# Three TensorE steps placed one chunk later, and a last store split by rows over two queues

## The chip, the cores and the metric

One core of one Trainium2 chip runs the whole program. The metric is the device time of one execution in microseconds (us); less is better. The kernel before was timed in three runs, and one further execution was recorded by the profiler.

## What is computed

Four residual stages on x of shape 4 x 512 x 512 (batch, tokens, features), all in fp32. Cut to what matters:

```python
x = x + gelu(_layernorm(x) @ ((w1.T @ w2.T) * sparse_mask) + b2)          # stage 1
x = x + ffn(_layernorm(x))                                               # stage 2
x = x + attention(_layernorm(x))        # stage 3: softmax(q k^T) v, then Wo
x = x + ffn(_layernorm(x))                                               # stage 4

def ffn(x):
    dots = softmax(x @ centroids.T / 0.1)       # 64 clusters, per token
    hits = dots > 0.01
    query_sel = any(hits, axis=1)               # per token
    cluster_sel = any(hits, axis=0)             # over ALL tokens of ALL batches
    row_sel = cluster_sel[assignments]          # per output feature
    return where(query_sel[:, None] & row_sel[None, :], x @ weight.T + bias, 0)
```

In stages 2 and 4 the line with `cluster_sel` matters most: no output of the stage can be finished before the cluster probabilities of every token are known.

## The kernel before

Tokens lie on the 128 partitions. There are 4 batches of 4 token tiles; a tile "b.t" is 128 tokens x 512 features. Each fp32 product is made of three matmuls on a high and a low part of its operands (hi*hi, lo*hi, hi*lo; `products`, line 1012). A tile's 512 x 512 product is cut by its contraction into four chunks of 128, so one chunk is three matmuls of 128x512. The steps of every engine stand in hand-written lists (`PE_ORDER`, `ACT_ORDER`, `DVE_ORDER`, `POOL_ORDER`, and `SP_ORDER` and `AS_ORDER` for the DMA issues of SyncE and ScalarE). Each engine works its own list strictly in order, and a step first waits on semaphores for what it reads and for the buffer it writes. `dn4.2.1.c3` is chunk 3 of the stage 4 product of tile 2.1; `c20` means chunks 2 and 0.

PSUM is split in two rotations of four banks each: `t_bank` for transposes and the masks, `m_bank` for products. A new tile takes the bank of the tile four places earlier in its rotation and waits until that one has been read (`bank_for`, line 1043). In stage 4 the tiles take `m_bank` in the order dn4.2.3, cl4.3, dn4.2.1, dn4.3.0, dn4.3.2, so dn4.3.2 waits for `blend4.2.3`, the VectorE step that reads dn4.2.3 (line 977).

The choice of clusters runs once in stage 2 and once in stage 4, through all engines. For the last batch (3) it is:

- `cl.3` (PE, line 1197): logits against the centroids; `lgev.3` (ACT, line 681): copy out of PSUM to `lg`;
- `tc.3` (PE, line 1119): four transposes of `lg`;
- `logit`, `lmax` (DVE, lines 930 to 937): sum of parts and maximum; `cexp` (ACT, line 703): four exponentials; `prob` (DVE, lines 944 to 954); `best1` (DVE, line 959): the maximum over all batches;
- `bestT` (PE, line 1124): its transpose; `csel` (DVE, lines 965 and 966): the chosen clusters;
- `mask.2` (PE, line 1144) in stage 2; `tmask.4` and `masks.4` (PE, line 1138) in stage 4: the mask of the output features, in PSUM. `tmask.4` is read by VectorE, and `masks.4` is copied by `rows4` (ACT, line 713) to SBUF for Pool.

PE works chunks of products between these steps.

In stage 4 a finished product is blended (`blend4`, DVE, line 977) with what has been prepared in `y_tok`, and then the mask is applied. Twelve tiles get it from VectorE with one `out` step (copy_predicated, line 1001), after Pool has added x to `y_tok` (`xb`, line 559). The tiles in `BY_POOL` (four: 1.3, 2.3, 3.2 and 2.2) get it from Pool instead, with two steps, `pm` (multiply, line 565) and `pa` (add, line 570), and no `xb`. The last tile, 3.3, is worked in two column halves (`dn4h`, `blend4h`, `outh`, lines 988 and 994).

Each tile is stored by one DMA of 256 KB once it is finished; tile 3.3 by two of 128 KB, one for each column half (`storeh`): the first issued by ScalarE (line 763), the second by SyncE (line 391). The last DMA in ScalarE's list is the store of tile 2.2 (line 769). SyncE then waits for all stores (line 434).

Of the kernel before, what the change touches and what calls it, by code (L numbers as in the profile page):

```python
# [24 lines left out]
M_BANKS = 4  # L25
WARM = 12

BY_POOL = {(1, 3), (2, 3), (3, 2), (2, 2)}

SQUARED = {2, 3, 4}  # L30

# [11 lines left out]
y1.3.3.c1 dn2.1.1.c02 y1.3.3.c3 dn2.1.3.c30 tc.2.1 y1.3.2.c1 y1.3.3.c20 y1.3.2.c3 dn2.1.1.c3 y1.3.2.c2  # L43
dn2.1.3.c1 T.x2.2.0 dn2.1.1.c1 dn2.1.3.c2 T.x2.2.2 y1.3.2.c0 y1.3.1.c2 T.x2.2.3 y1.3.1.c13 T.x2.2.1 y1.3.0.c1
y1.3.1.c0 y1.3.0.c302 T.x2.3.3 cl2.2.h01 T.x2.3.2 T.x2.3.1 dn2.2.3.c0 dn2.3.3.c3 dn2.2.3.c3 T.x2.3.0 tc.2.2
dn2.3.3.c1 dn2.2.3.c21 dn2.2.0.c2 cl2.3.h0 cl2.3.h1 dn2.2.2.c3 tc.2.3 dn2.2.2.c1 dn2.2.0.c1 dn2.2.2.c2
dn2.2.0.c03 dn2.3.3.c20 dn2.2.2.c0 bestT.2 dn2.3.1.c2 mask.2 dn2.2.1.c1 dn2.3.2.c3 dn2.3.1.c03 dn2.2.1.c2
dn2.3.2.c20 dn2.3.1.c1 dn2.3.2.c1 dn2.2.1.c0 T.x3.0.3 dn2.3.0.c13 T.x3.0.0 dn2.3.0.c0 T.x3.0.2 dn2.3.0.c2
T.x3.0.1 dn2.2.1.c3 k.0.h1 k.0.h0 q.0.h0 q.0.h1 v.0.h1 T.x3.1.3 v.0.h0 sc.0.0 T.x3.1.2 T.x3.1.1 sc.0.2 T.x3.1.0
# [6 lines left out]
T.p.3.3 wo.2.3 cl4.1.h01 wo.2.2 dn4.1.3.c0 tc.4.1 wo.2.0 dn4.1.0.c32 T.p.3.0 dn4.1.3.c1 dn4.1.0.c0 T.v.3.0  # L56
T.p.3.1 dn4.1.2.c3 dn4.1.3.c32 dn4.1.2.c102 dn4.1.0.c1 T.x4.2.2 T.x4.2.3 T.x4.2.0 wo.2.1 pv.3.h01 dn4.1.1.c012
wo.3.2 wo.3.0 dn4.1.1.c3 T.x4.2.1 wo.3.3 T.x4.3.0 T.x4.3.2 wo.3.1 cl4.2.h01 T.x4.3.1 T.x4.3.3 tc.4.2 dn4.2.3.c2
cl4.3.h0 dn4.2.1.c1 cl4.3.h1 dn4.2.1.c2 tc.4.3 dn4.2.1.c3 dn4.2.3.c1 dn4.2.1.c0 dn4.3.0.c2 dn4.2.3.c0 dn4.3.0.c0
dn4.2.3.c3 dn4.3.0.c31 bestT.4 dn4.3.2.c2 tmask.4 masks.4 dn4.3.2.c031 dn4.2.2.c0123 dn4.3.1.c0123 dn4.2.0.c0123  # L60
dn4h.3.3.0 dn4h.3.3.1
"""

# [45 lines left out]
rden.3 blend4.1.3 lo.p.3.0 lo.p.3.1 x3.2.1 blend4.1.0 blend4.1.2 lo.x4.2.3 olo.3 lo.x4.2.2 lo.x4.2.0 x3.3.2  # L109
x3.3.0 blend4.1.1 lo.x4.2.1 x3.3.3 lo.x4.3.2 x3.3.1 lo.x4.3.0 lo.x4.3.1 logit.4.2 lmax.4.2 lo.x4.3.3 prob.4.2  # L110
logit.4.3 lmax.4.3 prob.4.3 best1.4 blend4.2.3 csel.4 blend4.2.1 blend4.3.0 out.0.1 out.0.0 out.1.1 out.1.0
blend4.3.2 out.0.2 out.0.3 blend4.2.2 out.2.1 out.3.0 out.1.2 blend4.3.1 out.3.1 blend4.2.0 out.2.0
blend4h.3.3.0 outh.3.3.0 blend4h.3.3.1 outh.3.3.1
"""

# [8 lines left out]
bo.0.2 bo.0.1 masked.3.2 bo.0.0 bias2.3.3 bo.0.3 bias2.3.1 masked.3.3 rstd.3.3.3 masked.3.1 rstd.3.3.0 bo.1.0  # L124
rstd.3.3.2 bo.1.1 bo.1.2 rstd.3.3.1 bo.1.3 bo.2.1 bo.3.0 rstd.4.0 xb.0.1 bo.2.0 bo.2.3 xb.0.3 xb.0.2 xb.0.0
rstd.4.1 bo.2.2 bo.3.2 bo.3.3 xb.1.1 bo.3.1 xb.1.2 xb.1.0 rstd.4.2 rstd.4.3 xb.2.1 xb.3.0 xb.2.0 xb.3.3 xb.3.1
pm.1.3 pa.1.3 pm.2.3 pa.2.3 pm.3.2 pa.3.2 pm.2.2 pa.2.2
"""

SP_ORDER = """  # L130
load.x0.0 load.w2.0 load.x0.1 load.x0.2 load.w1.1 load.x0.3 load.w2.1 load.w2.2 load.w1.2 load.w1.3 load.w2.3
load.ffn.1 load.ffn.0 load.cen load.ffn.2 load.sparse.0 load.ffn.3 load.sparse.1 load.sparse.2 load.sparse.3
load.small load.x.1 load.b2 load.xt.1 load.x.3 load.late load.x.2 load.bias load.xt.2 load.xt.3 store.0.1
store.1.1 store.0.2 store.2.1 store.1.2 store.3.1 store.2.0 storeh.3.3.1
"""


# [1 line left out]


AS_ORDER = """
store.0.0 store.1.0 store.0.3 store.1.3 store.3.0 store.2.3 store.3.2 storeh.3.3.0 store.2.2
"""

def steps_of(text):
# [63 lines left out]
def program(nc, x_d, xt_d, w1_d, w2t_d, b2_d, sparse_d, wqkv_d, bqkv_d, wo_d, bo_d, ffn_d, fb_d, cen_d,  # L209
            assign_d, out_d):  # L210
    ctx = ExitStack()
    with ctx:
# [162 lines left out]
        @block.sync  # L375
        def _(sp):
            rows_of = lambda d: d.rearrange("(c p) n -> p c n", p=P)
            for kind, key in SP_STEPS:
                if kind == "store":
                    b, t = key  # L380
                    if key in BY_POOL:
                        sp.wait_ge(*done_at("pa", key))
                    else:
                        sp.wait_ge(*done_at("out", key))
                    sp.dma_start(out_d[b, t * P:(t + 1) * P, :], x_tok[:, b * TPB + t, :]).then_inc(stored, 16)
                    continue
                if kind == "storeh":
                    b, t, h = key
                    cols = slice(h * D // 2, (h + 1) * D // 2)
                    sp.wait_ge(*done_at("outh", key))  # L390
                    sp.dma_start(out_d[b, t * P:(t + 1) * P, cols], x_tok[:, b * TPB + t, cols]).then_inc(stored, 16)
                    continue
                what = key[0]
                if what in ("w2", "w1"):
                    c = key[1]
                    dst, src = (w2_raw, w2t_d) if what == "w2" else (w1_raw, w1_d)
                    sp.dma_start(dst[:, c, :], src[c * P:(c + 1) * P, :]).then_inc(ld[key], 16)
                elif what == "x0":
                    t = key[1]
                    sp.dma_start(x_tok[:, t, :], x_d[0][t * P:(t + 1) * P, :]).then_inc(ld[key], 16)  # L400
                elif what == "sparse":
                    c = key[1]
                    sp.dma_start(sparse[:, c, :], sparse_d[c * P:(c + 1) * P, :]).then_inc(ld[key], 16)
                elif what == "b2":
                    sp.dma_start(b2[:, :], b2_d.rearrange("(a n) -> a n", a=1).broadcast_to([P, D])).then_inc(ld[key], 16)
                elif what == "cen":
                    sp.dma_start(cen_raw, cen_d).then_inc(ld[key], 16)
                elif what == "ffn":
                    c = key[1]
                    sp.dma_start(ffn_raw[:, c, :], ffn_d[c * P:(c + 1) * P, :]).then_inc(ld[key], 16)  # L410
                elif what == "x":
                    b = key[1]
                    sp.dma_start(x_tok[:, b * TPB:(b + 1) * TPB, :], rows_of(x_d[b])).then_inc(ld[key], 16)
                elif what == "xt":
                    b = key[1]
                    if b == 1:
                        sp.wait_ge(*done_at("T", *[("x1", 0, t) for t in every]))
                    elif b == 2:
                        sp.wait_ge(*done_at("flo"))
                    else:  # L420
                        sp.wait_ge(*done_at("xlo", *[(1, t) for t in every]))
                    sp.dma_start(xt_raw[b % 2][:, :, :], rows_of(xt_d[b])).then_inc(ld[key], 16)
                elif what == "small":
                    sp.dma_start(bqkv[:, :], bqkv_d.rearrange("(j p) -> p j", p=P),
                                  allow_slow_non_contiguous=True).then_inc(ld[key], 16)
                    sp.dma_start(assign, assign_d.rearrange("(a n) -> a n", a=1).broadcast_to([P, D])).then_inc(ld[key], 16)
                elif what == "bias":
                    sp.dma_start(bias_f[:, :], fb_d.rearrange("(a n) -> a n", a=1).broadcast_to([P, D])).then_inc(ld[key], 16)
                    sp.dma_start(bo[:, :], bo_d.rearrange("(a n) -> a n", a=1).broadcast_to([P, D])).then_inc(ld[key], 16)
                elif what == "late":  # L430
                    sp.wait_ge(*done_at("alo"))
                    sp.dma_start(wqkv_raw, rows_of(wqkv_d)).then_inc(ld[key], 16)
                    sp.dma_start(wo_raw, wo_d).then_inc(ld[key], 16)
            sp.wait_ge(stored, 16 * sum(kind in ("store", "storeh") for kind, key in SP_STEPS + AS_STEPS))
# [138 lines left out]
        def _(act):  # L573
# [670 lines left out]
```

## Time and profile before

| | us |
|---|---|
| median of three runs | 275.42 (275.40 to 275.84) |
| the profiled execution's own time | 275.24 |
| its span | 273.4 |
| TensorE busy | 268.8 (98% of the span) |
| VectorE busy | 192.2 (70%) |
| ScalarE busy | 177.0 (65%) |
| Pool busy | 163.8 (60%) |

The profile is of one execution. Its instruction rows start at zero at the start of the span. The span is 1.84 us shorter than the execution's own time. The granted TensorE clock is 9 tenths or more in all 40 slices, and 0.999 in the mean. All DMA traffic lies in the first third (loads) and in the last three slices (stores). TensorE's ends are modelled, because its matmuls are pipelined, so the starts of its rows are the better guide: neighbouring rows overlap, and what is read here is the distance from one start to the next.

### The profile page before, as it was taken

To read this page: it belongs to the slowest core of one execution; us is meant where nothing else is said; L and a number is where in the kernel's file an instruction comes from. 1 tells how busy PE (TensorE), PEld (TensorE's weight loads), DVE (VectorE), ACT (ScalarE), POOL (GpSimd) and SP (SyncE) were. 2 spreads that over 40 slices of the span, in tenths; PEclk is the share of its full clock that TensorE was granted. 3 is DMA by queue.
4 is the path that set the end of the run, shared out by engine and by line. 5 is a ranking of instruction groups with operands and counts; after the bars stand their busy time and mean duration, and the time that the engine had idled before them with its cause. 6 is when DMAs were issued, how large, how long until landed. Compare 5 with 4: busy or idle time off the path is not lost.

```text
span 273.4 us, 4428 instructions
## 1 busy us (share of the span) xinstructions
PE 268.8 (98%) x1397; PEld 225.6 (82%) x1397; DVE 192.2 (70%) x406; ACT 177.0 (65%) x359; POOL 163.8 (60%) x196
## 2 busy tenths in 40 slices
PE   8999999999999999999999999999999999999995
PEld 8787888888888888788988888888888888887784
DVE  3988988605935867794478796788447584875994
ACT  3855886455477786448889988779544747577500
POOL 4883988265395491189896993990541247102795
PEclk9999999999999999999999999999999999999999
DMA  7999064800000000000000000000000000000096
GB/s 253 372 362 326 14 219 167 305 4 2 0 0 0 2 0 2 0 2 0 2 0 0 1 4 0 0 2 0 2 2 0 0 2 0 1 2 0 36 361 220
DMA packets 10247, 18.25 MB, mean 67 GB/s; under 512 B 1200, under 2 KB 1968, under 8 KB 10224
## 3 DMA queue, kind: packets, MB, share of 16 engines
q1 hardware_dynamic: 8784, 15.47, 16.2%
q10 hardware_dynamic: 1440, 2.49, 2.5%
q8 instruction: 12, 0.20, 0.3%
q14 instruction: 11, 0.09, 0.1%
HBM read 13.76 MB, written 4.19 MB: 66 GB/s over the span
## 4 chain that ended last, share of the span: by engine, by line
PE 96%; DMA 1%; DVE 1%; POOL 1%; issue 0%; ACT 0%; DVEq 0%; POOLq 0%
PE m_bank L1018 76%; PE t_bank L1113 12%; PE m_bank L1197 6%; PE t_bank L1119 1%; DMA x_tok<-in_L_attn_a_x 1%; PE m_bank L1073 1%; ACT xn_odd L613 0%; PE t_bank L1138 0%; DVE st L817 0%; POOL rstd L471 0%; POOL ve L470 0%; DVE y_tok L988 0%; DVE x_tok L994 0%; PE m_bank L1144 0%; PE t_bank L1124 0%
## 5 line engine op out<-in xcount | busy, mean ns | idle before, releaser
L1018 PE MATMUL m_bank<-ffn_hi,even_hi 128*128 128x512 f32 x96 | 38.9, 406 | 0.0
L1018 PE MATMUL m_bank<-ffn_lo,even_hi 128*128 128x512 f32 x96 | 37.6, 392 | 0.0
L1018 PE MATMUL m_bank<-ffn_hi,even_lo 128*128 128x512 f32 x96 | 37.4, 390 | 0.0
L602 ACT ACTIVATE ones_and_squares<-x_tok,mv 128x512 bf16<-128x512 f32 x44 | 31.6, 717 | 4.1 <-DVE x_tok L921 3.7
L559 POOL TENSOR_TENSOR y_tok<-y_tok,x_tok 128x512 f32<-128x512 f32 x12 | 15.3, 1289 | 25.6 <-ACT y_tok L755 25.6
L539 POOL TENSOR_TENSOR y_tok<-y_tok,bias_f 128x512 f32<-128x512 f32 x16 | 20.6, 1295 | 16.2 <-ACT y_tok L696 16.2
L467 POOL TENSOR_SCALAR ve<-mv 128x1 f32<-128x1 f32 (+1 forms) x20 | 5.3, 264 | 37.9 <-ACT ones_and_squares L602 36.9
L824 DVE TENSOR_TENSOR even_lo<-t_bank,even_hi 128x512 fp32r<-128x512 f32 x24 | 16.2, 684 | 12.8 <-ACT even_hi L645 12.6
L471 POOL TENSOR_TENSOR rstd<-ve,half 128x1 f32<-128x1 f32 (+1 forms) x31 | 23.5, 758 | 2.6
L824 DVE TENSOR_TENSOR odd_lo<-t_bank,odd_hi 128x512 fp32r<-128x512 f32 x28 | 18.8, 686 | 6.4 <-ACT odd_hi L645 6.2
L1018 PE MATMUL m_bank<-odd_hi,wqkv_hi 128*128 128x512 f32 (+1 forms) x60 | 21.5, 358 | 0.0
L1018 PEld LDWEIGHTS m_bank<-ffn_lo,even_hi 128*128 128x128 f32 x96 | 18.0, 188 | 3.9
L1018 PE MATMUL m_bank<-odd_lo,wqkv_hi 128*128 128x512 f32 (+1 forms) x60 | 20.9, 349 | 0.0
L553 POOL TENSOR_TENSOR x_tok<-x_tok,bo 128x512 f32<-128x512 f32 x16 | 20.9, 1322 | 0.0
L1018 PE MATMUL m_bank<-odd_hi,wqkv_lo 128*128 128x512 f32 (+1 forms) x60 | 20.8, 347 | 0.0
L1018 PEld LDWEIGHTS m_bank<-ffn_hi,even_lo 128*128 128x128 f32 x96 | 18.1, 189 | 3.1
L1018 PEld LDWEIGHTS m_bank<-ffn_hi,even_hi 128*128 128x128 f32 x96 | 18.1, 188 | 3.0
L613 ACT ACTIVATE xn_odd<-x_tok,ve,rstd 128x512 f32<-128x512 f32 x20 | 16.1, 811 | 5.8 <-POOL ve L474 5.8
L1018 PE MATMUL m_bank<-attn_hi,odd_hi 128*128 128x512 f32 x48 | 19.5, 406 | 0.0
L1018 PE MATMUL m_bank<-attn_lo,odd_hi 128*128 128x512 f32 x48 | 18.8, 392 | 0.0
L1018 PE MATMUL m_bank<-attn_hi,odd_lo 128*128 128x512 f32 x48 | 18.7, 390 | 0.0
L645 ACT ACTIVATE even_hi<-t_bank 128x512 fp32r<-128x512 f32 x24 | 13.8, 595 | 6.8 <-PE t_bank L1113 6.8
(191 smaller groups left out, 784.8 us busy)
## 6 DMA issues: line engine op xcount, KB each, us to landing
x_tok<-in_L_attn_a_x SPq DMA_DIRECT2D x3, 1024.0 KB, 9.8
xn_odd<-in_L_attn_a_xt SPq DMA_DIRECT2D x2, 1024.0 KB, 7.3
out<-x_tok ACTq DMA_DIRECT2D x8, 256.0 KB, 2.2
out<-x_tok SPq DMA_DIRECT2D x7, 256.0 KB, 2.2
x_tok<-in_L_attn_a_x SPq DMA_DIRECT2D x4, 256.0 KB, 4.1
w_raw<-in_L_attn_a_w SPq DMA_DIRECT2D x4, 256.0 KB, 5.0
xt_other<-in_L_ffn_weight SPq DMA_DIRECT2D x4, 256.0 KB, 5.9
y_tok<-in_L_attn_a_sparse_mask SPq DMA_DIRECT2D x4, 256.0 KB, 6.5
```

What stands on the lines that cost most here:

```text
L467: link(pool.tensor_scalar(ve[:, i:i + k], mv[:, i:i + k, 1], 1.0 / D ** 3, EPS, ALU.mult, ALU.add))
L471: ins = pool.tensor_tensor(rstd[:, i:i + k], ve[:, i:i + k], half[:, 0:k], ALU.pow)
L539: pool.tensor_tensor(y_tok[:, n, :], y_tok[:, n, :], bias_f[:, :], ALU.add).then_inc(done[kind], 1)
L553: pool.tensor_tensor(x_tok[:, n, :], x_tok[:, n, :], bo[:, :], ALU.add).then_inc(done[kind], 1)
L559: pool.tensor_tensor(y_tok[:, n, :], y_tok[:, n, :], x_tok[:, n, :], ALU.add).then_inc(done[kind], 1)
L602: act.activation(squares, x_tok[:, n, :], ACT.Square, bias=sum_of(*key), scale=-float(D), accum_out=mv[:, i, 1:2]).then_inc(done[kind], 1)
L613: act.activation(xn_odd[:, t, :], x_tok[:, n, :], ACT.Identity, bias=nbias[:, i:i + 1], scale=rstd[:, i:i + 1]).then_inc(done[kind], 1)
L645: act.activation(split_of(what, b, t)[0], bank_view(what, bank_of("T", *key)), ACT.Copy).then_inc(done[kind], 1)
L824: dve.tensor_tensor(lo, bank_view(what, bank_of("T", *key)), f32(hi), ALU.subtract).then_inc(done[kind], 1)
L1018: ins = pe.matmul(bank, a, w, start=(first and n == 0), stop=(last and n == count - 1))
L1113: ins = pe.transpose(bank[:, c * r:(c + 1) * r], blk, ident[0:r, 0:r])
L1197: ins = pe.matmul(bank[:, tokens], cen_hl[:, c, :], a[:, c, tokens], start=(c + h == 0), stop=(c == KC - 1 and h == 1))
```

## The change

- `tc.2.3` comes one chunk later: behind `dn2.2.2.c1` instead of ahead of it.
- `tc.4.3` comes one chunk later: behind `dn4.2.1.c3` instead of ahead of it.
- `tmask.4` and `masks.4` come one chunk later: behind chunks 2 and 0 of dn4.3.2 instead of behind chunk 2 alone.
- Tile 2.2 leaves `BY_POOL`. Pool loses `pm.2.2` and `pa.2.2` and gets `xb.2.2`, ahead of `pm.1.3`; VectorE gets `out.2.2`, ahead of `blend4.2.0`. Its store goes from the end of ScalarE's list into SyncE's list, and the store of tile 3.1 goes the other way.
- The second column half of tile 3.3 is stored by two DMAs of 64 KB, of 64 rows each: the upper on SyncE's queue, the lower on ScalarE's. Both wait for the same VectorE step, `outh.3.3.1`.

```diff
-BY_POOL = {(1, 3), (2, 3), (3, 2), (2, 2)}
+BY_POOL = {(1, 3), (2, 3), (3, 2)}
 # PE_ORDER
-dn2.3.3.c1 dn2.2.3.c21 dn2.2.0.c2 cl2.3.h0 cl2.3.h1 dn2.2.2.c3 tc.2.3 dn2.2.2.c1 dn2.2.0.c1 dn2.2.2.c2
+dn2.3.3.c1 dn2.2.3.c21 dn2.2.0.c2 cl2.3.h0 cl2.3.h1 dn2.2.2.c3 dn2.2.2.c1 tc.2.3 dn2.2.0.c1 dn2.2.2.c2
 dn2.2.0.c03 dn2.3.3.c20 dn2.2.2.c0 bestT.2 dn2.3.1.c2 mask.2 dn2.2.1.c1 dn2.3.2.c3 dn2.3.1.c03 dn2.2.1.c2
...
-cl4.3.h0 dn4.2.1.c1 cl4.3.h1 dn4.2.1.c2 tc.4.3 dn4.2.1.c3 dn4.2.3.c1 dn4.2.1.c0 dn4.3.0.c2 dn4.2.3.c0 dn4.3.0.c0
-dn4.2.3.c3 dn4.3.0.c31 bestT.4 dn4.3.2.c2 tmask.4 masks.4 dn4.3.2.c031 dn4.2.2.c0123 dn4.3.1.c0123 dn4.2.0.c0123
+cl4.3.h0 dn4.2.1.c1 cl4.3.h1 dn4.2.1.c2 dn4.2.1.c3 tc.4.3 dn4.2.3.c1 dn4.2.1.c0 dn4.3.0.c2 dn4.2.3.c0 dn4.3.0.c0
+dn4.2.3.c3 dn4.3.0.c31 bestT.4 dn4.3.2.c20 tmask.4 masks.4 dn4.3.2.c31 dn4.2.2.c0123 dn4.3.1.c0123 dn4.2.0.c0123
 dn4h.3.3.0 dn4h.3.3.1
 # DVE_ORDER
-blend4.3.2 out.0.2 out.0.3 blend4.2.2 out.2.1 out.3.0 out.1.2 blend4.3.1 out.3.1 blend4.2.0 out.2.0
+blend4.3.2 out.0.2 out.0.3 blend4.2.2 out.2.1 out.3.0 out.1.2 blend4.3.1 out.3.1 out.2.2 blend4.2.0 out.2.0
 # POOL_ORDER
-pm.1.3 pa.1.3 pm.2.3 pa.2.3 pm.3.2 pa.3.2 pm.2.2 pa.2.2
+xb.2.2 pm.1.3 pa.1.3 pm.2.3 pa.2.3 pm.3.2 pa.3.2
 # SP_ORDER
-store.1.1 store.0.2 store.2.1 store.1.2 store.3.1 store.2.0 storeh.3.3.1
+store.1.1 store.0.2 store.2.1 store.1.2 store.2.2 store.2.0 storer.3.3.0
 # AS_ORDER
-store.0.0 store.1.0 store.0.3 store.1.3 store.3.0 store.2.3 store.3.2 storeh.3.3.0 store.2.2
+store.0.0 store.1.0 store.0.3 store.1.3 store.3.0 store.2.3 store.3.1 store.3.2 storeh.3.3.0 storer.3.3.1
 # in SyncE's program; ScalarE's has the same with act for sp
+                if kind == "storer":
+                    b, t, r = key
+                    rows_r = slice(r * P // 2, (r + 1) * P // 2)
+                    sp.wait_ge(*done_at("outh", (b, t, 1)))
+                    sp.dma_start(out_d[b, t * P + r * P // 2:t * P + (r + 1) * P // 2, D // 2:D],
+                                 x_tok[rows_r, b * TPB + t, D // 2:D]).then_inc(stored, 16)
+                    continue
```

## Rows read from the trace of the kernel before

**Rows 1.** The page's shares of the chain of work that ended last, by engine.
```profile
PE 96%; DMA 1%; DVE 1%; POOL 1%; issue 0%; ACT 0%; DVEq 0%; POOLq 0%
```

**Rows 2.** That chain in order of time: start, length (us), what, instructions.
```profile
249.37 6.15 PE m_bank L1018 x27
```

**Rows 3.** Timeline of TensorE, stage 2: start, length (us), line, operation, shapes.
```profile
107.96 0.39 PE L1018 MATMUL m_bank<-ffn_lo,even_hi 128*128 128x512 f32 x1
108.44 0.63 PE L1119 MATMUL t_bank<-ident,lg 128*128 128x128 f32 x4
...
114.14 0.39 PE L1018 MATMUL m_bank<-ffn_lo,even_hi 128*128 128x512 f32 x1
114.44 0.27 PE L1124 MATMUL t_bank<-ident,best 128*64 128x128 f32 x1
...
115.45 0.47 PE L1144 MATMUL m_bank<-onehot,csel 128*128 128x512 f32 x1
```

**Rows 4.** Timelines of VectorE and ScalarE, stage 2; bracket: idle before, and what ended it.
```profile
109.17 0.69 DVE L930 TENSOR_REDUCE cl<-t_bank 128x256 f32<-128x512 f32 x1 [0.40 <-PE t_bank L1119]
...
112.02 0.42 DVE L944 TENSOR_REDUCE csum<-ce 128x4 f32<-128x256 f32 x1 [0.17 <-ACT ce L703]
...
113.67 0.62 DVE L959 TENSOR_REDUCE best<-best 128x64 f32<-128x256 f32 x1
...
115.07 0.28 DVE L966 TENSOR_SCALAR csel<-t_bank 64x128 fp32r<-64x128 f32 x1
...
110.55 1.44 ACT L703 ACTIVATE ce<-cl,ncmx,rstd 128x64 f32<-128x64 f32 x4 [2.26 <-DVE ncmx L937]
```

**Rows 5.** Timeline of TensorE, stage 4.
```profile
248.27 0.39 PE L1018 MATMUL m_bank<-ffn_lo,even_hi 128*128 128x512 f32 x1
248.74 0.63 PE L1119 MATMUL t_bank<-ident,lg 128*128 128x128 f32 x4
...
255.36 0.27 PE L1124 MATMUL t_bank<-ident,best 128*64 128x128 f32 x1
...
255.73 0.39 PE L1018 MATMUL m_bank<-ffn_hi,odd_lo 128*128 128x512 f32 x1
255.96 0.40 PE L1018 MATMUL m_bank<-ffn_lo,odd_hi 128*128 128x512 f32 x1
256.42 0.70 PE L1138 MATMUL t_bank<-onehot,csel 128*128 128x512 f32 x2
256.96 0.40 PE L1018 MATMUL m_bank<-ffn_hi,odd_hi 128*128 128x512 f32 x1
```

**Rows 6.** Timeline of VectorE, stage 4, around the same steps.
```profile
254.60 0.74 DVE L977 SCALAR_TENSOR_TENSOR y_tok<-m_bank,rq,y_tok 128x512 f32<-128x512 f32 x1
...
255.99 0.28 DVE L966 TENSOR_SCALAR csel<-t_bank 64x128 fp32r<-64x128 f32 x1
...
257.52 2.59 DVE L1001 COPY_PREDICATED x_tok<-t_bank,y_tok 128x512 f32<-128x512 int32 x4
```

**Rows 7.** TensorE's weight loads in the list of waits: us in total, times, longest.
```profile
PEld m_bank L1018 <- DVE y_tok L977: 0.2, 1, 0.2
```

**Rows 8.** Timeline of VectorE, the last 6 us.
```profile
267.40 0.75 DVE L977 SCALAR_TENSOR_TENSOR y_tok<-m_bank,rq,y_tok 128x512 f32<-128x512 f32 x1 [1.09 <-PE m_bank L1018]
```

**Rows 9.** Timelines of Pool, and of ScalarE's and SyncE's DMA issues, near the end.
```profile
254.86 5.05 POOL L559 TENSOR_TENSOR y_tok<-y_tok,x_tok 128x512 f32<-128x512 f32 x4 [2.83 <-ACT y_tok L755]
...
270.43 0.42 ACTq L769 DMA_DIRECT2D out<-x_tok  x1
...
271.33 0.33 SPq L391 DMA_DIRECT2D out<-x_tok  x1
```

**Rows 10.** DMA issues: queue, count, KB each, median us from issue to landing.
```profile
out<-x_tok SPq DMA_DIRECT2D x7, 256.0 KB, 2.2
...
out<-x_tok ACTq DMA_DIRECT2D x1, 128.0 KB, 2.1
out<-x_tok SPq DMA_DIRECT2D x1, 128.0 KB, 1.7
```

More of the change, by code:

```diff
@@ L433, in _ @@
                     sp.dma_start(wo_raw, wo_d).then_inc(ld[key], 16)
-            sp.wait_ge(stored, 16 * sum(kind in ("store", "storeh") for kind, key in SP_STEPS + AS_STEPS))
+            sp.wait_ge(stored, 16 * sum(kind in ("store", "storeh", "storer") for kind, key in SP_STEPS + AS_STEPS))
         @block.gpsimd
@@ L763, in _ @@
                     act.dma_start(out_d[b, t * P:(t + 1) * P, cols], x_tok[:, b * TPB + t, cols]).then_inc(stored, 16)
+                    continue
+                if kind == "storer":
+                    r = key[2]
+                    rows_r = slice(r * P // 2, (r + 1) * P // 2)
+                    act.wait_ge(*done_at("outh", (b, t, 1)))
+                    act.dma_start(out_d[b, t * P + r * P // 2:t * P + (r + 1) * P // 2, D // 2:D],
+                                  x_tok[rows_r, b * TPB + t, D // 2:D]).then_inc(stored, 16)
                     continue
```

## The prediction

> **What bounds the kernel.** I read the shares of the chain of waits first: TensorE holds 96% of what ended last [rows 1], so a change gains or costs what it does to TensorE's list, plus what it does to the tail behind the last matmul. Then the chain in order of time, for the price of a matmul: 27 take 6.15 us [rows 2], 0.228 us each, 0.68 us for a chunk of three. A distance above 0.23 us between two starts on TensorE is therefore a wait. Then the timelines of TensorE around the moved steps, with those of VectorE and ScalarE beside them. For the tail, VectorE's last idle times and the issues and landings of the stores.
>
> **Moving tc.2.3.** Before `tc.2.3` TensorE goes 0.48 us from start to start, 107.96 to 108.44 [rows 3]: 0.25 us of wait. One chunk later the wait is over long before the step is reached. So the move takes away 0.25 us, and I count 0.02 more for the restart of the pipeline (an estimate; behind the mask in stage 4 the restart shows as 0.08, below): 0.27 us. But `tc.2.3` itself now starts at 107.96 + 0.23 + 0.68 = 108.87, which is 0.43 us later than now; its end, without the slow restart, about 0.41 later.
>
> What hangs on it? I follow the steps to `best1`. `logit` sat idle 0.40 us until the transposes were done, the exponentials sat idle 2.26 us until the maximum was there, `csum` waited for the exponentials, and `best1` ends at 113.67 + 0.62 = 114.29 [rows 4]. Every link starts when the one before ends, and no engine does foreign work that would absorb a shift. `bestT.2` starts at 114.44, 0.15 us behind the end of `best1`; the matmul before it started at 114.14, a distance of 0.30 where 0.23 is free [rows 3]. So TensorE is already waiting for this chain now, by 0.07 us: the chain has no slack. With `tc.2.3` 0.41 us later, `best1` ends at 114.70 and `bestT.2` can start at 114.85. TensorE's work up to `bestT.2` is the same as now, only its order differs, so without a wait it would be there at 114.37 - 0.27 = 114.10. It waits 0.75 us.
>
> Behind it, `csel` ends at 115.07 + 0.28 = 115.35 and `mask.2` starts at 115.45 [rows 3, 4]. Both follow `bestT.2`, so they go to 115.76 and 115.86. The work before and after `mask.2` is the same list as now, so what TensorE carries on from there is 0.41 us. The move that takes a wait of 0.27 us away puts one of 0.68 more in its place. Bounds: there is a second small wait behind `bestT.2` now, for a bank; if only this one were absorbed and `mask.2` did not follow `csel`, +0.25; if `mask.2` starts 0.15 behind `csel` as `bestT.2` does behind `best1`, +0.46. I take +0.41.
>
> Nothing gives this back later: TensorE is bound from there on, and all that the other engines do for stages 3 and 4 starts from its products or from this mask.
>
> **Moving tc.4.3.** The same picture: 248.27 to 248.74 is 0.47 us, a wait of 0.24 [rows 5], and 0.27 with the restart (estimate as above). `tc.4.3` would start at 248.27 + 0.23 + 0.68 = 249.18, 0.44 us later than now, its end 0.41 later. Here `bestT.4` has a little slack in front, but the step behind it has none. Chunk 2 of dn4.3.2 needs the bank that `blend4.2.3` frees, and `blend4.2.3` stands behind `best1` in VectorE's list. It ends at 254.60 + 0.74 = 255.34 [rows 6], and the second matmul of the chunk starts at 255.73 [rows 5], 0.39 us behind. The list of waits has TensorE's weight loads idle for 0.2 us on just this release already now [rows 7]: TensorE and the blend are level, and there is no slack. After the move `blend4.2.3` ends at 255.75 and that matmul starts at 256.14: +0.41 us at the same work, the 0.27 us gained at `tc.4.3` already counted in.
>
> **Moving tmask.4 and masks.4.** Now `tmask.4` starts 0.46 us behind the matmul before it, 255.96 to 256.42, since `csel` ends only at 255.99 + 0.28 = 256.27; then two mask matmuls take 0.54 us to the next chunk at 256.96 instead of 0.46 [rows 5, 6]. The waits are 0.23 and 0.08: 0.31 us. With chunk 0 ahead of them, and TensorE 0.41 us later, the mask comes at 256.14 + 0.46 + 0.68 = 257.28; `csel`, which now waits for `blend4.2.3` ahead of it on VectorE instead of for `bestT.4`, ends at about 256.31. No wait is left. So stage 4 gives +0.41 - 0.31 = +0.10 us. Bounds: 0 if the bank is free 0.1 earlier than the shift says, +0.20 if the waits at the masks go only in part.
>
> **Who waits for the later mask.** `tmask.4` ends at about 257.28 + 0.40 = 257.68. VectorE's first `out` starts at 257.52 now [rows 6], so VectorE is put back by about 0.2 us. It also gets `out.2.2`: four such steps take 2.59 us [rows 6], 0.65 each. Together 0.85 us, hidden in the 1.09 us that VectorE sits idle before `blend4.2.0` [rows 8]. If that cover were gone, each 0.1 us over it would be 0.1 us of time. `masks.4` is read by Pool only after its `xb` steps.
>
> **Pool.** It loses two steps and gets `xb.2.2`: four of these take 5.05 us, 1.26 each [rows 9], so its end comes 1.26 us earlier, less the 0.41 us by which its `xb` group starts later. `xb.2.2` would be done at 254.86 + 0.41 + 5 x 1.26 = 261.6, and VectorE comes to `blend4.2.2`, which then waits for it, after six `out` steps and a blend: 257.7 + 6 x 0.65 + 0.74 = 262.3. Hidden, by some 0.7 us. Behind `blend4.2.2` all remaining `out` steps are queued. On ScalarE's list store 3.1 stands behind store 2.3, which waits for Pool; it is no late one: Pool is through with tile 2.3 two steps, 2.5 us, before its last tile.
>
> **The last store.** Now: issue at 271.33 [rows 9], landing 1.7 us later [rows 10]. The store of tile 2.2 is issued at 270.43, only 0.9 us ahead [rows 9], and leaves that place. 256 KB land in 2.2 us, 128 KB in 1.7 or 2.1 [rows 10]: half the bytes save between 0.1 and 0.5 us, so if each half of 64 KB moved alone, up to about 0.25 us. But the two halves move at the same time, to the same memory, and the later one ends the kernel; the nearest row for 128 KB in one go is the 1.7 itself, a gain of 0. I take -0.05, for the store of 2.2 that is no longer beside it, with -0.25 and +0.1 as ends.
>
> The Trainium skill, DMA: Bandwidth & Descriptors, section "Rules for kernel authors", speaks against this part: two transfers to disjoint partition halves are not worth it, because they run on the same DMA engines and serialize. By that rule this term is 0, and by halves that move side by side it would be -0.25; no row of before has two halves of one tile in flight at once, so it stays untested here.
>
> **The sum.** 0.41 + 0.10 - 0.05 = +0.46 us. On the profiled execution, 275.24, that gives 275.70; the median of the runs is 0.18 higher, and on it the forecast is 275.42 + 0.46 = 275.9.
>
> **Rivals.**
> - The chains have slack that I don't see, and the waits just go: -0.27 - 0.27 - 0.31 - 0.05 = -0.90 us, 274.5. For it: the three waits are real, and nothing of their cause, the wait for a copy or a choice just made, is left after a chunk. Against it: `bestT.2` waits today, and `blend4.2.3` is level with TensorE today. It would need `best1` ready 0.7 us sooner behind `tc` than it is. 0.17.
> - The last store lands later, not earlier. The lower half goes through ScalarE's queue, where 128 KB took 2.1 us instead of 1.7 [rows 10]. If the lower half meets data of the first column half or of tile 3.2 still in flight, that queue ends the kernel: +0.4 in place of -0.05, +0.91 in all, 276.3. It decides only if stores are still moving when the data of the halves do, that is between their issue and their landing. Against it: that one stood between two stores of 256 KB, and the nearest of these goes away. 0.18.
> - The change doesn't do what it says in the tail, because VectorE takes over as the bound with `out.2.2`: only if the 0.85 us exceed 1.09, a price of 0.1 or 0.2; inside the range of the main case.
>
> **How the numbers follow.** Main case 0.60, with its own range 275.4 to 276.1 from the ends of the three terms. Faster rival 0.17, slower rival 0.18, 0.05 for neither. A measurement of this kernel can tell about 0.2%, 0.55 us, from no change: 274.87 and 275.97 are the borders. Of the main case about 0.3 lies above 275.97, so slower is 0.18 + 0.18 = 0.36, faster is 0.17, and the rest, 0.47, is within. The range must reach both rivals to leave out no more than 0.2: 274.5 to 276.4.
>
> **What would show it.** In the profile after: the distance before both `tc` steps falls from 0.47 or 0.48 to 0.23; before `bestT.2` it rises from 0.30 to about 1.0; the second matmul behind `bestT.4` starts 0.39 us behind the end of a `blend4.2.3` that comes 0.4 us later; no wait before `tmask.4`; VectorE idles about 0.3 us before `blend4.2.0`; the last store lands 1.6 to 1.7 us behind its issue on both queues. I am wrong if `bestT.2` starts less than 5.9 us behind `tc.2.3`, if TensorE has waits left in stage 3 that soak up 0.4 us, or if a half lands past 2 us.

## The result, and the profile after

The changed kernel is slower: 278.12 us in four runs against 275.51, a ratio of 1.0083 (95% interval 1.0063 to 1.0103). Timed again in twelve runs it took 277.45 against 275.52, a ratio of 1.0060 (1.0039 to 1.0080). The ratio with its interval is reckoned apart from the medians and isn't always their quotient (for e8 below the medians give +0.69 us, the ratio +0.25); amounts in us are differences of medians. I had forecast 275.9 and a range of 274.5 to 276.4; both times lie above the range. The profiled execution after took 278.14 us, with a span of 276.3 against 273.4.

The page after, in the shares of the chain that ended last, by engine (before: [rows 1]):

```profile
PE 91%; DVE 4%; DMA 2%; issue 1%; ACT 1%; SPq 0%; DVEq 0%; ACTq 0%
```

TensorE lost 5% of the chain to VectorE, the DMAs and ScalarE. Line numbers after are up to 14 higher than before. I divide the 2.9 us by the distance of like instructions in the two timelines, from front to back.

**The head.** TensorE's timeline and VectorE's, changed kernel:

```profile
8.97 1.20 PE L1087 MATMUL m_bank<-w2t_lo,even_hi 128*128 128x512 f32 x4 [0.87 <-DVE w2t_lo L801]
...
6.62 0.69 DVE L831 BATCH_NORM_STATS2 st<-x_tok 128x6 f32<-128x512 f32 x1 [1.21 <-DMA x_tok<-in_L_attn_a_x]
```

The same four matmuls start at 8.09 before. VectorE waited 1.21 us for the second load of x, and 0.88 us are lost before any edit is reached. This is not the change: see the table of all profiles below.

**Stage 2** (before: [rows 3, 4]). Changed kernel, TensorE, then VectorE:

```profile
109.58 0.39 PE L1032 MATMUL m_bank<-ffn_lo,even_hi 128*128 128x512 f32 x1
109.81 0.60 PE L1133 MATMUL t_bank<-ident,lg 128*128 128x128 f32 x4
...
114.83 0.39 PE L1032 MATMUL m_bank<-ffn_lo,even_hi 128*128 128x512 f32 x1
115.76 0.27 PE L1138 MATMUL t_bank<-ident,best 128*64 128x128 f32 x1 [0.54 <-DVE best L973]
...
116.78 0.47 PE L1158 MATMUL m_bank<-onehot,csel 128*128 128x512 f32 x1
...
115.02 0.59 DVE L973 TENSOR_REDUCE best<-best 128x64 f32<-128x256 f32 x1
```

The distance in front of `tc.2.3` has fallen from 0.48 to 0.23, as it should. `bestT.2` starts 5.95 us behind `tc.2.3` (6.00 before), with one chunk less in between: the distance in front of it has grown from 0.30 to 0.93 us, of which the profile calls 0.54 idle. `mask.2` is 1.33 us later than before, of which 0.93 was there when the last matmul ahead of both edits started (108.89 against 107.96): stage 2 costs 0.40 us.

**Stage 4** (before: [rows 5, 6]). TensorE, VectorE and Pool, changed kernel:

```profile
250.49 0.60 PE L1133 MATMUL t_bank<-ident,lg 128*128 128x128 f32 x4
...
257.33 0.27 PE L1138 MATMUL t_bank<-ident,best 128*64 128x128 f32 x1 [0.78 <-DVE best L973]
257.90 0.50 PE L1032 MATMUL m_bank<-ffn_hi,odd_hi 128*128 128x512 f32 x1 [0.30 <-DVE y_tok L991]
258.23 0.39 PE L1032 MATMUL m_bank<-ffn_hi,odd_lo 128*128 128x512 f32 x1
...
259.16 0.40 PE L1032 MATMUL m_bank<-ffn_lo,odd_hi 128*128 128x512 f32 x1
259.40 0.62 PE L1152 MATMUL t_bank<-onehot,csel 128*128 128x512 f32 x2
259.86 0.40 PE L1032 MATMUL m_bank<-ffn_hi,odd_hi 128*128 128x512 f32 x1
...
252.37 0.98 DVE L951 SCALAR_TENSOR_TENSOR ncmx<-cmx,rstd 128x4 f32<-128x4 f32 x1
...
257.10 0.74 DVE L991 SCALAR_TENSOR_TENSOR y_tok<-m_bank,rq,y_tok 128x512 f32<-128x512 f32 x1
...
252.04 1.29 POOL L566 TENSOR_TENSOR y_tok<-y_tok,x_tok 128x512 f32<-128x512 f32 x1 [4.06 <-ACT y_tok L762]
```

The masks have lost their wait (0.24 us from start to start), and 1.08 us of idle time have appeared at `bestT.4` and the bank behind it. From the last matmul ahead of the edits (249.57 against 248.27: +1.30) to the same work behind the masks (259.86, which has one chunk more done than 256.96, so 259.17: +2.21), stage 4 costs 0.91 us. The odd row is `ncmx`: a VectorE step on 128 x 4 numbers that takes 0.98 us instead of 0.16. It starts 0.33 us behind Pool's `xb.2.1` and ends 0.02 us behind it. Before, the order was the other way round, VectorE, then Pool:

```profile
250.66 0.16 DVE L937 SCALAR_TENSOR_TENSOR ncmx<-cmx,rstd 128x4 f32<-128x4 f32 x1
...
250.74 1.29 POOL L559 TENSOR_TENSOR y_tok<-y_tok,x_tok 128x512 f32<-128x512 f32 x1 [4.07 <-ACT y_tok L755]
```

**The tail** (before: [rows 9, 10]). VectorE's last step, the issues, and the DMA rows, changed kernel:

```profile
273.08 0.44 DVE L1008 COPY_PREDICATED x_tok<-t_bank,y_tok 128x256 f32<-128x256 int32 x1
...
273.55 0.52 SPq L397 DMA_DIRECT2D out<-x_tok  x1
...
273.55 0.56 ACTq L776 DMA_DIRECT2D out<-x_tok  x1
...
out<-x_tok ACTq DMA_DIRECT2D x1, 128.0 KB, 3.1
out<-x_tok SPq DMA_DIRECT2D x1, 64.0 KB, 2.0
out<-x_tok ACTq DMA_DIRECT2D x1, 64.0 KB, 2.3
```

The halves take 0.52 and 0.56 us to issue instead of 0.33, and land 2.0 and 2.3 us behind instead of 1.7. From the end of the last VectorE step to the end of the span it is 2.8 us now, 2.1 before: 0.7 us. Sum: 0.88 + 0.40 + 0.91 + 0.7 = 2.9 us, the whole difference of the spans.

### The profile page after: what moved, and what is told of

It reads as the page before. It is cut to its first block, busy times and chain, and to the rows that moved or that the text cites. A ratio compares the mean times of both kernels' runs of the same rounds, so it can differ in the third digit from the quotient of the medians.

```text
span 276.3 us, 4430 instructions
## 1 busy us (share of the span) xinstructions
PE 268.1 (97%) x1397; PEld 224.5 (81%) x1397; DVE 194.2 (70%) x407; ACT 177.2 (64%) x359; POOL 163.0 (59%) x195
## 4 chain that ended last, share of the span: by engine, by line
PE 91%; DVE 4%; DMA 2%; issue 1%; ACT 1%; SPq 0%; DVEq 0%; ACTq 0%
PE m_bank L1032 71%; PE t_bank L1127 11%; PE m_bank L1211 5%; DMA x_tok<-in_L_attn_a_x 2%; PE t_bank L1133 1%; ACT ce L710 1%; PE m_bank L1087 1%; DVE cl L944 1%; DVE st L831 1%; DVE ncmx L951 0%; DVE csum L958 0%; DVE cmx L949 0%; DVE best L968 0%; DVE y_tok L991 0%; DVE w2t_lo L801 0%
## 5 line engine op out<-in xcount | busy, mean ns | idle before, releaser
L566 POOL TENSOR_TENSOR y_tok<-y_tok,x_tok 128x512 f32<-128x512 f32 x13 | 16.6, 1296 | 26.8 <-ACT y_tok L762 26.8
```

What stands on the lines that cost most here:

```text
L566: pool.tensor_tensor(y_tok[:, n, :], y_tok[:, n, :], x_tok[:, n, :], ALU.add).then_inc(done[kind], 1)
```

## The experiments

For every profiled execution I read the same three quantities: the start of the four `w2t_lo` matmuls (head), TensorE's own part of the edit (like instructions ahead of the edited steps and behind them, against before), and the time from the end of the last VectorE step to the end of the span (tail).

| kernel | median us, ratio (95% interval) | head | TensorE | tail |
|---|---|---|---|---|
| before | 275.5 | 8.09 | | 2.10 |
| after | 278.12, 1.0083 (1.0063 to 1.0103) | 8.97 | +1.3 | 2.78 |
| e1 tc.2.3 | 275.88, 1.0013 (1.0003 to 1.0023) | 8.30 | +0.4 | 2.24 |
| e2 tc.4.3 | 276.79, 1.0047 (1.0035 to 1.0060) | 8.23 | +0.9 | 2.36 |
| e3 masks | 275.23, 0.9994 (0.9986 to 1.0003) | 8.67 | -0.3 | 2.23 |
| e4 stores | 276.07, 1.0017 (1.0008 to 1.0026) | 8.74 | 0 | 2.66 |
| e5 after again | 277.45, 1.0060 (1.0039 to 1.0080) | 8.24 | +1.2 | 2.68 |
| e6 after, Pool waits | 276.62, 1.0035 (1.0015 to 1.0055) | 8.35 | +0.5 | 2.79 |
| e7 halves only | 276.44, 1.0024 (1.0002 to 1.0045) | 8.15 | 0 | 2.66 |
| e8 Pool move only | 276.21, 1.0009 (0.9989 to 1.0029) | 8.28 | 0 | 2.73 |
| e9 qb swapped | 275.93, 1.0011 (0.9997 to 1.0024) | 8.10 | +0.5 | 2.22 |
| e10 one matmul | 275.21, 0.9990 (0.9977 to 1.0002) | 8.39 | -0.3 | 2.27 |
| e11 halves, one queue | 276.15, 1.0023 (1.0011 to 1.0036) | 8.09 | 0 | 2.97 |
| e12 one store less | 275.22, 0.9990 (0.9978 to 1.0002) | 8.08 | 0 | 2.14 |
| e13 column quarters | 275.39, 1.0001 (0.9991 to 1.0012) | 8.90 | 0 | 2.22 |
| e14 more work, both | 277.79, 1.0085 (1.0068 to 1.0101) | 8.59 | +2.0 | 2.65 |
| e15 more work, stage 4 | 275.38, 1.0003 (0.9990 to 1.0017) | 8.19 | -0.5 | 2.54 |

A difference of some tenths between two whole spans can't be put down to an edit from one profile of each. In e8 and e12 TensorE also loses 0.3 and 0.4 us where nothing was edited, at 159 us and at 24 us. The six kernels with the stores of before and no more work in stage 4 (before, e1, e2, e3, e9, e10) have tails of 2.10 to 2.36, so the tail before is the lowest of its kind, and the cost of a tail of 2.7 is 0.3 to 0.6 us.

The head varies between 8.08 and 8.97 over kernels that don't differ there at all; the changed kernel has 8.97 in one profile and 8.24 in the other. So the 0.88 us of the head belong to that one execution and not to the change, and a rival by which every differing kernel pays it falls with e1, e7, e9, e11 and e12.

**The four edits one at a time.** e1 to e3 each make one of the moves in TensorE's list; e4 makes the rest of the change.

```diff
 # e1
-dn2.2.2.c3 tc.2.3 dn2.2.2.c1
+dn2.2.2.c3 dn2.2.2.c1 tc.2.3
 # e2
-dn4.2.1.c2 tc.4.3 dn4.2.1.c3
+dn4.2.1.c2 dn4.2.1.c3 tc.4.3
 # e3
-bestT.4 dn4.3.2.c2 tmask.4 masks.4 dn4.3.2.c031
+bestT.4 dn4.3.2.c20 tmask.4 masks.4 dn4.3.2.c31
```

> Only tc.2.3 is moved one chunk later; all else as before. Theory A (the chain behind tc.2.3 has no slack): +0.41 us, the distance from tc.2.3 to bestT.2 stays near 6.0 us and the wait in front of bestT.2 rises to about 1.0 us from start to start. Rival B (the head of the program is slower by 0.9 us in every kernel that differs from the one before, through the loads alone): +1.3 us here. Rival C (the waits just go): -0.27 us.

> Only tc.4.3 is moved one chunk later. Theory A2 (the 128x4 VectorE step ncmx now starts behind the start of Pool's xb.2.1 and is held until Pool is through, about 0.98 us long instead of 0.16): about +1.0 us (1.23 at the bank of dn4.3.2, less some 0.2 of the waits at the masks). Rival (the plain shift of the prediction, nothing held): about +0.2 us and ncmx 0.16 us long. Rival B (slow head): 0.9 more than either.

> Only tmask.4 and masks.4 are moved one chunk later. Theory A: -0.3 us, the 0.46 us in front of tmask.4 fall to 0.23 and nothing comes in its place, because nothing that VectorE does next needs the mask before 257.5. Rival: 0, because VectorE's out steps start 0.2 to 0.4 us later and reach the last half. Rival B (slow head): +0.6 us.

> Only the second part of the change: tile 2.2 masked by VectorE, its store moved, and the last half stored by two row halves on two queues. TensorE's list as before. Theory A3 (two issues at the same instant hold each other up, 0.52 to 0.56 us instead of 0.33, and the halves land 2.0 to 2.3 us behind instead of 1.7): +0.5 us, all of it behind the last VectorE step. Theory of the prediction: -0.05 us. Rival B (slow head): 0.9 more.

Measured: +0.34, +1.25, -0.31 and +0.53 us on the medians, 1.8 together. All four times came as theory A, A2 and A3 had them, e2 0.25 us higher. The interval of e3 includes 1, so its gain rests on its timeline, where TensorE is 0.3 us earlier behind the masks. e2's timelines show the long `ncmx` again, with the Pool step that started ahead of it:

```profile
251.23 0.99 DVE L937 SCALAR_TENSOR_TENSOR ncmx<-cmx,rstd 128x4 f32<-128x4 f32 x1
...
250.89 1.30 POOL L559 TENSOR_TENSOR y_tok<-y_tok,x_tok 128x512 f32<-128x512 f32 x1 [4.07 <-ACT y_tok L755]
```

**Is that the whole change?** e5 is the changed kernel again.

> The changed kernel itself, against the kernel before on one chip in five rounds. If its cost is the sum of what the four single edits measured (+0.34, +1.25, -0.31, +0.53): 277.3 us, +1.8. If 0.9 us of its profile, the slower head through the loads, belong to the kernel and not to the single execution: 278.1 us, +2.6.

277.45 us, +1.93: nearer the sum of the four edits (277.3) than 278.1. Its interval, 1.0039 to 1.0080, leaves out +2.6 us (1.0094), but it overlaps with that of the first measurement (1.0063 to 1.0103).

**Does Pool hold `ncmx` up?** e6 and e9 test it from both sides. e6 takes the overlap out of the changed kernel; e9 puts it into the kernel before, where no step of TensorE is moved.

```diff
 # e6, Pool's program
                 elif kind == "xb":
...
+                    if key == (2, 1):
+                        pool.wait_ge(*done_at("lmax", (4, NB - 1)))
 # e9, ScalarE's list
-lgev.4.3 qb.2.0 qb.2.1 cexp.4.3
+lgev.4.3 qb.2.1 qb.2.0 cexp.4.3
```

> The changed kernel with one wait added: Pool starts xb.2.1 only once lmax of the last batch (with it ncmx) is done. Theory A2 (ncmx is held by Pool's step): ncmx back to 0.16 us, the stage 4 part falls from +0.92 to +0.10, 0.8 us faster than the changed kernel. Rival (something else in the chain is slow, ncmx is only where it shows): the same time as the changed kernel or slower, by the wait.

> The kernel before, no TensorE step moved; only ScalarE prepares tile 2.1 (qb.2.1) ahead of tile 2.0 (qb.2.0), so that Pool's xb.2.1 starts some 0.65 us earlier, at about 250.1 instead of 250.74, ahead of ncmx at 250.66 instead of behind it. Theory A2 (whichever of the two starts first holds the other up): ncmx is 0.7 us long instead of 0.16, the whole chain and TensorE behind blend4.2.3 come 0.6 us later, +0.5 us with no wait or step added. Rival (ncmx was long for the shift of tc.4.3): no change.

e6 takes 276.62 us, 0.83 less than e5 on the same chip, with `ncmx` at 0.16 us. VectorE and Pool, e6, then e9:

```profile
251.67 0.16 DVE L953 SCALAR_TENSOR_TENSOR ncmx<-cmx,rstd 128x4 f32<-128x4 f32 x1
...
251.91 1.29 POOL L568 TENSOR_TENSOR y_tok<-y_tok,x_tok 128x512 f32<-128x512 f32 x1 [4.63 <-DVE ncmx L953]
```

```profile
250.84 0.78 DVE L937 SCALAR_TENSOR_TENSOR ncmx<-cmx,rstd 128x4 f32<-128x4 f32 x1
...
250.31 1.30 POOL L559 TENSOR_TENSOR y_tok<-y_tok,x_tok 128x512 f32<-128x512 f32 x1 [3.46 <-ACT y_tok L755]
```

In e9 Pool starts 0.53 us ahead of `ncmx`, and `ncmx` takes 0.78 us and ends as Pool ends (251.62 and 251.61). TensorE pays 0.5 us. The ratio, 1.0011 or 0.3 us, agrees, but its interval includes 1, so e9 rests on its timeline; e6 has the time. The order of the two starts decides: adding a wait to Pool made the kernel faster by 0.8 us. The Trainium skill says in SBUF — State Buffer, section "Who interferes with whom", that a VectorE instruction with two inputs in SBUF contends with a GpSimd instruction that reads SBUF, and that the order of issue decides who blocks; that the first one holds the other out for its whole length it says of VectorE's modes on both ports. `ncmx` reads two SBUF tensors, and it behaves that way in e2, e5, e9 and the changed kernel, where it ends within 0.03 us of Pool's step. Whether a VectorE step that is first holds Pool up can't be seen here: in the kernel before the two overlap by 0.08 us only.

**Why does the tail cost?** e7 and e8 take the second part of the change apart; e11 and e13 vary the cut of the last half; e12 takes a store away from e8.

```diff
 # e7: stores as before, but
-storeh.3.3.1
+storer.3.3.0
-store.3.2 storeh.3.3.0 store.2.2
+store.3.2 storeh.3.3.0 store.2.2 storer.3.3.1
 # e8: BY_POOL, out, xb and all stores as in the change, but the last half in one DMA
-storer.3.3.0
+storeh.3.3.1
-storeh.3.3.0 storer.3.3.1
+storeh.3.3.0
 # e11: e7 with both halves in SyncE's list
 # e13: e7 with each piece 128 rows x 128 columns
+                    cols = slice(D // 2 + r * D // 4, D // 2 + (r + 1) * D // 4)
+                    sp.dma_start(out_d[b, t * P:(t + 1) * P, cols], x_tok[:, b * TPB + t, cols]).then_inc(stored, 16)
 # e12: e8 without store.2.3, so tile 2.3 of the output is never written (for this question only)
```

> The kernel before with only the last half stored as two row halves on two queues; Pool keeps tile 2.2, whose store stays the last but one on ScalarE's queue. Theory A3 (the halves themselves cost, by issuing at the same instant): +0.4 to +0.6 us, each issue 0.5 us long or more. Rival (it was the moved stores that filled the queues): -0.05 to +0.1 us, issues of 0.33 us.

> The kernel before with the last half stored as two row halves, both issued by SyncE one behind the other. If two issues at the same instant hold each other up: each issue is back to 0.33 us, data of the first half start 0.85 us behind its issue instead of 1.17, and the end is within 0.3 us of the kernel before. If small DMAs are slow by themselves: issues of 0.5 us here too, +0.5 us.

> The kernel before with the last half stored as two pieces of 64 KB on two queues as in e7, but cut by columns: 128 rows x 128 columns each. If it is the 64 rows that make the issue slow: issues of 0.33 to 0.42 us, data 0.85 us behind, +0.0 to +0.2 us. If it is the smaller piece: issues of 0.5 us and +0.5 us, as e7.

The issues of the last pieces, e11, then e13 (two queues), with e13's landings:

```profile
271.46 1.14 SPq L397 DMA_DIRECT2D out<-x_tok  x2
```

```profile
272.11 0.33 SPq L397 DMA_DIRECT2D out<-x_tok  x1
...
272.12 0.36 ACTq L775 DMA_DIRECT2D out<-x_tok  x1
...
out<-x_tok SPq DMA_DIRECT2D x1, 64.0 KB, 1.6
out<-x_tok ACTq DMA_DIRECT2D x1, 64.0 KB, 1.8
```

My theory A3, that two issues at the same instant hold each other up, falls with e11: one behind the other on one queue, they still take 0.57 us each (1.14 for the two). That they are simply small falls with e13: two issues at the same instant, 64 KB each, take 0.33 and 0.36 us if each piece keeps all 128 rows, and the kernel is back at the time of before (1.0001). It is the cut by rows: a store of 64 rows takes 0.51 to 0.57 us to issue. What in it is slow isn't shown. And even the good cut gains nothing.

> The kernel before with tile 2.2 masked by VectorE and the stores reordered as in the change, but the last half in one DMA on SyncE's queue. Theory A3: 0 to -0.1 us, landing 1.7 us behind the issue. Rival (the moved stores cost): +0.3 us or more, landing 2 us behind.

> The kernel of e8 (tile 2.2 on VectorE, last half in one DMA) without the store of tile 2.3, so a quarter of a megabyte of the output is not written. Theory A4 (one DMA engine is busy 1.7 us with fetching instructions and works off a backlog of stores that reaches the last half): no packets of the last half come late on one engine, it lands 1.7 to 1.8 us behind its issue instead of 2.3, 0.5 us faster than e8. Rival (the order of the stores or the queue they use makes the last one slow): still 2.2 to 2.3.

By its median and interval e8 is inconclusive; its profile isn't. The last half is one DMA as before, its issue takes 0.33 us, and it still lands late. The DMA rows and the busy share of the 16 DMA engines at the end, e8 (first the traffic from 267 us on):

```profile
q8 instruction: 1, 0.02, 1.3%
...
out<-x_tok SPq DMA_DIRECT2D x1, 128.0 KB, 2.3
...
272.75:273.00 0.25, 1.00 0.99 344
273.00:273.25 0.25, 1.00 0.22 70
273.25:273.50 0.25, 1.00 0.06 20
273.50:273.75 0.25, 1.00 0.07 25
```

The same for e12:

```profile
out<-x_tok SPq DMA_DIRECT2D x1, 128.0 KB, 1.7
...
272.50:272.75 0.25, 1.00 0.88 299
272.75:273.00 0.25, 1.00 0.69 230
273.00:273.25 0.25, 0.70 0.00 0
```

In e8 the share drops to 0.06 or 0.07, one engine of 16, for the last 0.5 us: one DMA engine is behind. What I take to have put it there is the packet of kind "instruction" (16 KB, a fetch of code): 1.3% of 16 engines over 8 us is 1.7 us on one engine, in the middle of the last stores. A store of 256 KB is 16 KB for each of 16 engines. In the kernel before the same fetch is there (1.4% of 7 us, 1.6 us on one engine), and all engines end together: the engine had caught up. The reordered list leaves it more to do behind the fetch. With one store less (e12) nothing is late, the last half lands in 1.7 us, and the tail is 2.14 us instead of 2.73. So less to store takes the backlog away. That the fetch starts it is read from the trace and not shown: e12 has the same packet, and no run moved the fetch. Nor does a run tell the new order of the stores from the other part of e8, tile 2.2 on VectorE.

Does the backlog end the changed kernel too? In e5 the share is 0.07 from 273.25 to 273.75, one engine again. Then it is 0.19 for 0.25 us and 0.94 and 0.91 after that: the engine is through before the data of the two row halves flow at full rate, 1.25 us behind their issue at 272.75. There the row cut alone sets the end. In the first profile the share is 0.07, 0.08 and 0.16 from 274.00 to 274.75, right up to the halves' data (0.84 after that), so the backlog may add some of the 0.1 us by which its tail is longer (2.78 against 2.68).

**Filling the waits without moving the chain.** e10 has the masks of e3, and lets the transposes run behind the first matmul of the next chunk, so that `tc` starts when it does in the kernel before. e15 adds more work between the links of stage 4, and e14 does so in stage 2 as well.

```diff
 # e10, in products(): dn2.2.2.c1 carries tc.2.3, dn4.2.1.c3 carries tc.4.3
                         n += 1
+                        if inside and n == 1:
+                            transpose_logits(inside)
 # e15, on top of e10 (PE, then DVE)
-dn4.3.0.c31 bestT.4 dn4.3.2.c20 tmask.4 masks.4 dn4.3.2.c31
+dn4.3.0.c31 dn4.3.2.c2 bestT.4 dn4.3.2.c03 tmask.4 masks.4 dn4.3.2.c1
-best1.4 blend4.2.3 csel.4
+blend4.2.3 best1.4 csel.4
 # e14, on top of e15
-bestT.2 dn2.3.1.c2 mask.2 dn2.2.1.c1 dn2.3.2.c3 dn2.3.1.c03
+dn2.3.1.c2 bestT.2 dn2.3.1.c0 dn2.2.1.c1 mask.2 dn2.3.2.c3 dn2.3.1.c3
```

> The stores as before; tmask.4 and masks.4 one chunk later as in the change; tc.2.3 and tc.4.3 only one matmul later: they run inside the chunk they stood in front of, behind its first matmul, so TensorE fills the 0.24 us wait with 0.23 us of work and the chains behind start when they do now. Theory A: -0.25 -0.25 -0.31 = -0.8 us, 274.7, faster than both kernels. Rival (a switch between products and transposes costs as much as it fills): -0.3 us, as the masks alone.

Measured: 275.21, no more than e3 alone. TensorE, stage 2, e10:

```profile
108.78 0.63 PE L1072 MATMUL t_bank<-ident,lg 128*128 128x128 f32 x4
...
114.27 0.39 PE L1027 MATMUL m_bank<-ffn_lo,even_hi 128*128 128x512 f32 x1
114.78 0.27 PE L1139 MATMUL t_bank<-ident,best 128*64 128x128 f32 x1
```

The wait ahead of `tc.2.3` is gone, and the distance ahead of `bestT.2` has grown from 0.30 to 0.51. `bestT.2` starts 6.00 us behind `tc.2.3`, as before. I had expected -0.8 us: wrong, for the same reason that made the move itself a loss. The wait was never TensorE's to save; `bestT` comes when the chain lets it.

> e10 (one matmul in front of the tc steps, masks a chunk later) and in both stages bestT one chunk later and the mask two; in stage 4 VectorE runs blend4.2.3 ahead of best1.4, so that the bank of dn4.3.2 is free earlier. If the chain from the logits to the mask is what TensorE waits for: the waits in front of bestT, the bank and the mask go too, -0.9 to -1.1 us against the kernel before, 274.5. Rival: stage 3 starts later by what the mask is late, and TensorE waits at the first T.x3 steps: -0.3 us as the masks alone, or worse.

> e14 without the edit of stage 2 (there only tc.2.3 is one matmul later, as in e10). By the chain theory -0.5 to -0.6 us, 275.0: the waits at the bank of dn4.3.2 and at the masks go, those of stage 2 stay. Rival (VectorE's later best1 makes the mask late for its out steps, which reach the last half): 0 or slower.

e14 takes 277.79 us. Stage 4 works as in e15, stage 2 doesn't: the mask comes at 117.24 instead of 115.45, what the other engines prepare for stage 3 comes later, and TensorE waits for ScalarE. These two waits don't exist in the kernel before. TensorE's timeline, e14, stage 3:

```profile
126.76 0.63 PE L1132 MATMUL t_bank<-ident,xn_odd 128*128 128x128 f32 x4 [0.72 <-ACT xn_odd L622]
...
130.73 0.38 PE L1027 MATMUL m_bank<-odd_hi,wqkv_hi 128*128 128x256 f32 x1 [1.32 <-ACT y_tok L705]
```

These two waits are 2.04 us; stages 2 and 3 together cost 2.5. This is the rival that I had given e14: work that fills the wait at `bestT.2` is work that stage 3 then lacks beside its chain.

e15 shows that the reading of stage 4 is right and that it still gives nothing. It takes 0.54 us off TensorE there; 0.44 is left at the last matmul, since its head happens to be 0.10 late. Yet the time is 275.38, as before: the tail is 2.54 us instead of 2.10. The last half's issue and landing, and the busy share of the DMA engines, e15:

```profile
270.89 0.33 SPq L400 DMA_DIRECT2D out<-x_tok  x1
...
out<-x_tok SPq DMA_DIRECT2D x1, 128.0 KB, 2.1
...
271.50:271.75 0.25, 1.00 1.01 377
271.75:272.00 0.25, 0.54 1.00 385
272.00:272.25 0.25, 0.50 0.98 336
272.25:272.50 0.25, 0.50 0.95 316
```

All 16 DMA engines are busy to 272.5. The store of tile 2.2, held to Pool's last tile, was issued at 270.56, only 0.33 us ahead of the last half instead of 0.9 [rows 9], and its 256 KB are in the way. With TensorE earlier and Pool not, the end moves onto Pool and its store; this is read from the trace, no run moved Pool's work in e15. No complete version beat the kernel before: e3 (0.9994) and e10 (0.9990) are the lowest, and the interval of each includes 1.

## Why the prediction was wrong

The sign was right and the size was not: I had +0.46 us, the changed kernel costs 1.9 (e5) to 2.6 us. Two steps of the prediction failed, one in the chain of stage 4 (0.82 us) and one at the last store (0.5 to 0.7 us).

- **tc.2.3: right.** Forecast +0.41; measured 0.40 in the timeline and +0.34 for e1 alone. The distance in front of `bestT.2` went from 0.30 to 0.93 us; I had about 1.0.
- **tc.4.3: the first step that failed.** I shifted the chain by 0.41 us and took each link's duration as fixed. The shift moved `ncmx` from 0.08 us ahead of a Pool step (250.66 and 250.74) to 0.33 behind it, and a link of 0.16 us became one of 0.98: +0.82. I wrote that no engine does foreign work that would *absorb* a shift, looked for this at VectorE's and ScalarE's rows, and never asked what foreign work could *stretch* a link, though that Pool step stood in the trace. My bounds for stage 4, 0 to +0.20, came from slack alone. The rest of the step was right: of the 0.91 us measured for stage 4, 0.09 are left without the collision, against +0.10 for `tc.4.3` and the masks together.
- **The masks: right.** Forecast -0.31; e3 measures -0.31 on the medians and -0.3 on its timeline.
- **What I hid behind idle time: right.** VectorE still idles 0.50 us before `blend4.2.0`, `blend4.2.2` doesn't wait for Pool, and e4 adds nothing to TensorE.
- **The last store: the second step that failed, wrong by sign.** Forecast -0.05, ends -0.25 and +0.1; measured +0.7 in the first profile, +0.58 in that of e5, +0.53 for e4 as a whole. My own sign for it, a half that lands past 2 us, came true (2.0 and 2.3). The cut into 64 rows is enough alone (e7 and e11, undone in e13), and so is one DMA engine's backlog under the new stores (e8, undone in e12). Their costs don't add: tails of 2.66 and 2.73 us alone, 2.66 to 2.79 together, since in e5 the engine has caught up when the late halves flow. My working had bytes and queues in it, and neither the number of rows nor the engines' state when the data come. "It is no late one", of store 3.1, looked at when it is issued, not at what is still to be moved behind it. The slower rival had the direction of the tail, with another mechanism: both queues are late, not ScalarE's alone.
- **The rule on halves.** The Trainium skill, DMA: Bandwidth & Descriptors, section "Rules for kernel authors", advises against two transfers to disjoint partition halves. The runs agree with the advice, and the price is more than the 0 that I worked out from it (e7, 1.0024). Of a cut by columns that rule doesn't speak; it came out at 1.0001 (e13).
- **The faster rival falls.** e10 removes the waits at both `tc` steps without delaying them, and gains nothing over e3.

The sum by the timelines: 0.40 + 0.91 + 0.7 = 2.0 us, against +1.93 for e5 and 1.8 for e1 to e4 added up. The spans of e5 and before differ by the same 2.0: 0.15 in the head, 1.27 from there to the last matmul, 0.58 in the tail. The first measurement, +2.6, lies 0.6 above that. Its profile lost 0.88 us in the loads at the head; whether the loads did the same in its other three runs can't be told, and this part stays open.

## What to carry to other kernels

A wait of the bounding engine in front of a step that a dependent chain hangs on isn't that engine's to save: look at where the chain comes back, and if the engine already waits there, leave the step alone. Before shifting a chain by some tenths of a us, compare the start of each of its small VectorE steps with the starts of Pool's steps nearby; if the shift turns the order round, a step of 0.16 us can take 0.8 to 1.0. If the last store is cut at all, keep all 128 rows in each piece, and look at the 16 DMA engines' share up to its landing: in e8 the store ended with the one engine that was behind.

## What the runs showed of the hardware that I had not expected

- A VectorE step on 128 x 4 numbers took 0.78 to 0.99 us when a Pool step on 128 x 512 had started 0.33 or 0.53 us ahead of it, and ended with it, to within 0.03 us (changed kernel, e2, e5, e9). When `ncmx` started 0.08 ahead of Pool, it took 0.16 us and Pool its usual 1.29 (before).
- A store of 64 rows x 256 columns took 0.51 to 0.57 us to issue, one of 128 rows x 128 columns, the same 64 KB, 0.33 to 0.36; they landed in 2.0 to 2.4 and in 1.6 to 1.8 us.
- One packet of kind "instruction", 16 KB, took 1.5 to 1.7 us of one DMA engine among the stores (before, e8, e12) and 1.1 in e5. In e8 one DMA engine of 16 worked 0.5 us longer than the others, and a store of 128 KB landed in 2.3 us instead of 1.7 (e12, one store less); that the packet is the cause isn't shown.
- The loads of x at the start differ by 0.9 us between executions: the same matmul starts at 8.08 to 8.97 us in the 17 profiles, with no edit ahead of it.
